# Moving the residual passes, the last two groups' order and the yr buffers in a fused attention and mixture-of-experts kernel

## What is computed

```python
h = _layernorm(x) * (1 + ca) + sa
q = h @ Wq;  Q = K = elu(q) + 1;  V = q / L
Z = 1 / (Q . Ksum + eps)
msg = (Q KV Z) * L @ Wm                       # linear attention, 8 heads of 16
a = h + _layernorm(msg, g1, b1)
a = a + _layernorm(relu(msg @ W1) @ W2, g2, b2)
x = x + ga * a
h = _layernorm(x) * (1 + cb) + sb
x = x + gb * experts(h)                       # 8 experts, top-512 tokens each, gelu FFN
```

## Times and profile before

| | us |
|---|---|
| median of 3 runs (310.49 to 312.85) | 312.84 |
| the profiled execution's own time | 311.66 |
| its span in the trace | 309.9 |

### The profile page before, as it was taken

How to read it: one execution, slowest core, us unless ns; L and a number is a source line. 1 busy time by engine, 2 the same in 40 slices (tenths; PEclk the granted TensorE clock), 3 DMA queues, 4 the chain that set the end, 5 groups by cost and what they waited for, 6 DMA issues and landing times.

```text
span 309.9 us, 4483 instructions
## 1 busy us (share of the span) xinstructions
PE 177.5 (57%) x1035; PEld 145.2 (47%) x1035; DVE 200.9 (65%) x701; ACT 98.5 (32%) x338; POOL 161.0 (52%) x229
## 2 busy tenths in 40 slices
PE   0878896596798895351112033527754574588730
PEld 0546684575586585351001022426644464577520
DVE  3789839949999988658897997013533253346660
ACT  1189843144265463115564002002221121222200
POOL 8645278917555334406991006770076665735552
PEclk9999997778699799555555555755995765758995
DMA  6940000000100000002662003432243333324210
GB/s 156 257 132 2 1 0 0 2 0 1 36 0 1 2 1 0 2 0 68 188 186 69 0 0 120 121 118 69 79 118 96 101 107 97 119 78 121 93 36 17
DMA packets 21721, 20.08 MB, mean 65 GB/s; under 512 B 2624, under 2 KB 19008, under 8 KB 21696
## 3 DMA queue, kind: packets, MB, share of 16 engines
q1 hardware_dynamic: 18144, 13.24, 14.7%
q0 software_dynamic: 2560, 6.30, 6.7%
q10 hardware_dynamic: 992, 0.27, 0.9%
HBM read 13.51 MB, written 6.29 MB: 64 GB/s over the span
## 4 chain that ended last, share of the span: by engine, by line
DVE 33%; PE 29%; another core or an unknown queue 13%; POOL 8%; issue 7%; ACT 6%; DMA 1%; DVEq 1%; POOLq 1%; ACTq 0%
PE pH L773 9%; DVE x_sb L965 6%; DVE hT L1044 5%; PE pQ L782 4%; POOL yr L244 3%; PE pH L675 3%; DVE bn L817 2%; ACT u L534 2%; PE pQ L668 2%; PE pQ L685 2%; POOL rs L244 2%; DVE xn L825 2%; PE pQ L567 2%; ACT x_sb L530 1%
## 5 line engine op out<-in xcount | busy, mean ns | idle before, releaser
L773 PE MATMUL pH<-x_sb,hid 128*128 (+1 forms) x156 | 35.9, 366 | 36.1 <-ACT x_sb L530 26.3
L373 POOL DMA_INDIRECT out_dram<-u,gidx x32 | 32.1, 1005 | 41.8 <-DVE u L1178 31.5
L369 POOL DMA_INDIRECT xn<-table_dram,gidx x32 | 33.6, 1051 | 33.2 <-DVE gidx L1138 23.8
L1166 DVE SCALAR_TENSOR_TENSOR h<-pQ,wslot,h 128x128 f32 (+1 forms) x39 | 13.7, 351 | 57.4 <-PE pQ L782 21.5
L773 PEld LDWEIGHTS pH<-x_sb,hid 128*128 128x128 f32 x156 | 27.1, 246 | 43.4 <-issue 43.4
L534 ACT ACTIVATE u<-pH 128x256 f32<-128x256 f32 x39 | 15.0, 384 | 80.7 <-remote 36.4
L782 PE MATMUL pQ<-ew,u 128*128 (+1 forms) x156 | 31.4, 337 | 3.9 <-issue 2.6
L782 PEld LDWEIGHTS pQ<-ew,u 128*128 128x128 f32 x156 | 27.6, 249 | 5.0 <-issue 4.7
L965 DVE SCALAR_TENSOR_TENSOR x_sb<-u,yr,x_sb 128x128 f32<-128x128 f32 x64 | 24.6, 445 | 4.4 <-POOL yr L244 4.1
L479 ACT ACTIVATE sqj<-pQ 128x128 bf16<-128x128 f32 x64 | 16.9, 278 | 28.4 <-POOL yr L244 12.3
L243 POOL TENSOR_SCALAR ve<-mv 128x4 f32<-128x4 f32 x16 | 3.3, 205 | 36.5 <-DVE mv L820 36.3
(11 more groups left out here) (275 smaller groups left out, 441.2 us busy)
## 6 DMA issues: line engine op xcount, KB each, us to landing
hid<-in_L_ffn_W_dram SPq DMA_DIRECT2D x39, 128.0 KB
x_sb<-in_L_attn_x_dram SPq DMA_DIRECT2D x8, 256.0 KB, 6.5
table_dram<-x_sb SPq DMA_DIRECT2D x8, 256.0 KB, 2.8
table_dram<-h SPq DMA_DIRECT2D x8, 256.0 KB, 2.3
ew<-in_L_ffn_W_dram SPq DMA_DIRECT2D x2, 512.0 KB, 7.6
xn<-table_dram,gidx POOLq DMA_INDIRECT x32
out_dram<-u,gidx POOLq DMA_INDIRECT x32
wmod_sb<-in_L_wmod_dram SPq DMA_DIRECT2D x1, 384.0 KB, 4.9
```

The costliest lines, as they stand in the source:

```text
L369: gp.indirect_dma_start(row[:, t % R, :], None, table[:, :], bass.IndirectOffsetOnAxis(gidx[:, t:t + 1], 0), bounds_check=B * L - 1, oob_i ...
L373: gp.indirect_dma_start(out.rearrange("b l d -> (b l) d"), bass.IndirectOffsetOnAxis(gidx[:, t:t + 1], 0), o_sb[:, t % RO, :], None, bound ...
L773: mm = te.matmul(pH[i % 2][:, f * P:(f + 1) * P], wcur[:, i % RW, f * P:(f + 1) * P], xt[:, bass.ds(i - e, 1), :], start=True, stop=True)
```

## The change

The residual passes are placed anew. POOL now does groups 0, 1, 2, 3, 4 and 7: acc(0) and acc(1) stand behind qprime(1), and then acc(2), acc(3), acc(4), acc(7) at the ends of steps 2 to 5. DVE does group 5 ahead of the last v_feat of the first stage and group 6 behind v_z(0). In the last steps DVE does x1(7) before xn3(6), POOL does yrs(7) before rs3(6), and PE does lg(6) before tx3(7). ssq, yv and yr have four buffers in place of two, with the waits to match.

```diff
-POOLACC = 5
+POOL_RES = (0, 1, 2, 3, 4, G - 1)
+RY = 4
...
             def acc(g):
                 b = g // GB
-                if g:
-                    gp.wait_ge(S["acc_done"], g)
+                k = POOL_RES.index(g)
+                if k:
+                    gp.wait_ge(S["acc_done"], k)
...
-            gp.wait_ge(S["rows_done"], 1)
-            gp.wait_ge(S["xn1"], G)
-            acc(0)
...
-                if g >= 2:
-                    gp.wait_ge(S["x1_done"], g - 1)
+                if g >= RY:
+                    gp.wait_ge(S["x1_done"], g - RY + 1)
...
             for s in range(G + 6):
                 if s < G:
                     qprime(s)
+                if s == G + 2:
+                    yrs(G - 1)
                 if 0 <= s - 4 < G:
                     rs3(s - 4)
-                if 0 <= s - 3 < G:
+                if 0 <= s - 3 < G - 1:
                     yrs(s - 3)
-                if s + 1 < POOLACC:
-                    acc(s + 1)
+                if s == 1:
+                    gp.wait_ge(S["rows_done"], 1)
+                    gp.wait_ge(S["xn1"], G)
+                    acc(0)
+                if 0 <= s - 1 < len(POOL_RES) - 1:
+                    acc(POOL_RES[s])
...
             def a_square(g, k, ready, done):
                 act.wait_ge(S[ready], g + 1)
-                if g >= 2:
-                    act.wait_ge(S["yr_done"], g - 1)
+                if g >= RY:
+                    act.wait_ge(S["yr_done"], g - RY + 1)
...
+                if s == G + 5:
+                    p_lg(G - 2)
                 if 0 <= s - 6 < G:
                     p_tx3(s - 6)
...
-                if 0 <= s - 7 < G:
+                if 0 <= s - 7 < G and s != G + 5:
                     p_lg(s - 7)
...
                 if s == G - 1:
                     v_kvt(0)
+                    v_acc(5)
...
-                if 1 <= s <= G - POOLACC:
-                    v_acc(POOLACC + s - 1)
+                if s == 0:
+                    v_acc(6)
+                if s == G + 3:
+                    v_x1(G - 1)
                 if 0 <= s - 5 < G:
                     v_xn3(s - 5)
-                if 0 <= s - 4 < G:
+                if 0 <= s - 4 < G - 1:
                     v_x1(s - 4)
```

More of the change, by code:

```diff
@@ L97, in build @@
         z = sb("z", [P, 2, GT * H]); qp = sb("qp", [P, 2, W]); qT = sb("qT", [P, 2, W])
-        hid = sb("hid", [P, 2, 2, W]); ssq = sb("ssq", [P, 2, 2 * GT]); yv = sb("yv", [P, 2, 2 * GT]); yr = sb("yr", [P, 2, 2 * GT])
+        hid = sb("hid", [P, 2, 2, W]); ssq = sb("ssq", [P, RY, 2 * GT]); yv = sb("yv", [P, RY, 2 * GT]); yr = sb("yr", [P, RY, 2 * GT])
         u1 = sb("u1", [P, 3, GT, D]); u2 = sb("u2", [P, 2, GT, D]); t2 = sb("t2", [P, GT, D]); t1 = sb("t1", [P, GT, D])
@@ L335, in yrs @@
                 gp.wait_ge(S["sq2"], g + 1)
-                if g >= 2:
-                    gp.wait_ge(S["x1_done"], g - 1)
-                rsqrt(yr[:, g % 2, :], ssq[:, g % 2, :], yv[:, g % 2, :], 1.0 / D, LN_EPS, 2 * GT).then_inc(S["yr_done"], 1)
+                if g >= RY:
+                    gp.wait_ge(S["x1_done"], g - RY + 1)
+                rsqrt(yr[:, g % RY, :], ssq[:, g % RY, :], yv[:, g % RY, :], 1.0 / D, LN_EPS, 2 * GT).then_inc(S["yr_done"], 1)
             def rs3(g):
@@ L475, in a_square @@
                 act.wait_ge(S[ready], g + 1)
-                if g >= 2:
-                    act.wait_ge(S["yr_done"], g - 1)
+                if g >= RY:
+                    act.wait_ge(S["yr_done"], g - RY + 1)
                 for t in range(GT):
                     last = act.activation(sqj[:, g % 2, k * GT + t, :], pQ[k][:, t * D:(t + 1) * D], ACT.Square,
-                                          accum_out=ssq[:, g % 2, k * GT + t:k * GT + t + 1])
+                                          accum_out=ssq[:, g % RY, k * GT + t:k * GT + t + 1])
                 last.then_inc(S[done], 1)
@@ L908, in v_kvt, with v_acc @@
                 dve.tensor_tensor(kvt[:, b, :], kv_bank(b), same16[:, :], ALU.mult).then_inc(S["kvt_done"], 1)
+            def v_acc(g):
+                b = g // GB
+                dve.wait_ge(S["rows_done"], 1)
+                link(dve.tensor_tensor(t2[:, :, :], xn[:, g], row4(rA[:, b, :]), ALU.mult))
+                link(dve.tensor_tensor(t2[:, :, :], t2[:, :, :], row4(rD[:, b, :]), ALU.add))
+                dve.tensor_tensor(bgroup(x_sb, g), bgroup(x_sb, g), t2[:, :, :], ALU.add).then_inc(S["acc_late"], 1)
+                dve.wait_ge(S["acc_late"], g - 4)
             for s in range(G + 1):
@@ L939, in v_relu @@
                 dve.tensor_scalar(hid[:, g % 2, 1, :], pH1[:, :], 0.0, None, ALU.max).then_inc(S["relu1"], 1)
[L941 to L946, removed]
             def v_u1(g):
@@ L959, in v_x1 @@
                 dve.wait_ge(S["yr_done"], g + 1)
-                if g < POOLACC:
-                    dve.wait_ge(S["acc_done"], g + 1)
+                if g in POOL_RES:
+                    dve.wait_ge(S["acc_done"], POOL_RES.index(g) + 1)
                 for u, n in ((u1[:, g % 3], 0), (u2[:, g % 2], GT)):
@@ L964, in v_x1 @@
                         x1 = x_sb[:, g * GT + t, :]
-                        last = dve.scalar_tensor_tensor(x1, u[:, t, :], yr[:, g % 2, n + t:n + t + 1], x1, ALU.mult, ALU.add)
+                        last = dve.scalar_tensor_tensor(x1, u[:, t, :], yr[:, g % RY, n + t:n + t + 1], x1, ALU.mult, ALU.add)
                     if n == 0:
```

## The result

| | before | changed |
|---|---|---|
| median of 20 runs, us | 312.71 (310.44 to 314.11) | 314.75 (312.90 to 316.78) |
| the profiled execution's own time, us | 311.66 | 314.16 |
| its span, us | 309.9 | 312.4 |
| DVE's mx starts (end of the middle stage), us | 137.22 | 139.12 |
| the experts' first gather on POOL starts, us | 187.39 | 189.09 |

The ratio of the changed kernel to the one before is 1.0076, with a 95% interval of 1.0049 to 1.0103: it is 2.0 us slower, which is less than 1%. The middle stage ends 1.9 us later. The search behind it takes 50.0 instead of 50.2 us, and the rest of the 2.5 us between the two spans lies in the experts' stage, 123.3 instead of 122.5 us. All ratios here leave out executions that took over 1.5% longer than the fastest of their kernel; in experiment E11 these are three of six.

The account below looks back on a forecast made before the run. The middle stage's chain of waits through DVE, POOL and PE was taken as the bound: start -2.8, passes beside x1 +6.4, tail -0.8 make +2.8 us, so 314.5 to 315.6, stated as 315.0 us; range 312.3 to 317.8 us.

Parts of the forecast that it names:

- the ring: Middle stage, DVE and POOL: x1(g), its stats, rs3(g) and yrs(g+1) wait in turn; what x1 takes, the ring takes.
- The passes behind yr(1) and yr(2) cost 6.4 us: Middle: x1(1) and x1(2) meet a pass on POOL and take 6.28 instead of 3.10 us each; bounds 6.2 to 6.5.
- The start gives 2.8 us: Up to x1(0): y2(0) ends at 64.3 us, as POOL takes back most of DVE's gain; bounds 1.1 to 5.1 us.
- the clock's return: Start, on PE: full clock returns 4 to 6 us after 56.6, so y2(0) ends at 64.0 to 65.1 us.
- acc(0) no longer beside DVE's pass costs nothing, the pass fits: First stage, DVE: group 5's pass takes 2.1 us within a 2.75 us wait for exp, without POOL's acc(0) beside it.
- The tail gives 0.8 us: Stage's end: x1(7) ends 2.7 us earlier, but PE's logit work at half clock keeps only 0.8; bounds 0 to 4.0.
- x1(7)'s start: Tail, on DVE: x1(7) starts at 123.8 instead of 126.56 us, within 0.1 us of u2(7)'s end.
- The four buffers do nothing: Buffers of ACT's squares and POOL's yrs: waits two groups back vanish, costed at nothing and gaining nothing.
- the slow clock: Rival on PE: the chain to y2(0) keeps its 7.60 us, the tail gives nothing; +5.3 us, 317.5 us; chance 0.20.
- the clock that stays up: Rival on PE: 2.4 GHz from tq(2) on; +0.5 us, 312.7 us, or 309.5 with a full-clock tail; chance 0.20.
- a ring that is bound elsewhere: Rival in the middle: POOL's yrs(2) waited for squares rather than rs3(1); time 312 us; chance 0.03.
- the ports held by DVE: Rival in the middle: x1's operations make POOL's passes wait, the middle costs nothing; about 309 us; chance 0.05.

Follow-up runs that it names:

- E11: The kernel before with only x1(7) ahead of xn3(6) and yrs(7) ahead of rs3(6); ratio to the kernel before 0.988.
- E1: The changed kernel without the residual passes of groups 4 and 7, so its output lacks them; ratio to the kernel before 0.985.
- E2: The changed kernel with POOL starting the passes of groups 4 and 7 only when x1(1), x1(2) are done; ratio to the kernel before 1.008.
- E7: The changed kernel with qp(4) to qp(7) waiting until x1(0) to x1(3) are done; ratio to the kernel before 1.001.
- E6: The changed kernel with POOL's pass of group 1 behind qp(2) and that of group 2 behind qp(3); ratio to the kernel before 0.996.
- E10: The changed kernel with acc(0) ahead of POOL's loop again, as in the kernel before; ratio to the kernel before 0.990.
- E4: The changed kernel with PE's tail order as before, tx3(7) ahead of lg(6); ratio to the kernel before 1.006.
- E5: The changed kernel with all three tail orders (DVE, POOL, PE) as before; ratio to the kernel before 1.014.
- E3: The changed kernel with two buffers for ssq, yv and yr instead of four; ratio to the kernel before 1.010.

## Why the prediction was right

The time, 314.75 us, lies 0.25 us from the 315.0 forecast, and the case is the forecast one. That it came so near is luck. The sum gave +2.8 us at the stage's end, where 1.9 us were measured: the start gave 1.1 us and a turn of the ring 0.4 us more than forecast, and the tail 0.7 us less. Outside the stage, where the forecast had nothing, another 0.6 us was added. What is more than luck is the largest term, the two passes beside x1, which came to within 0.1 us. Point by point:

- *The passes behind yr(1) and yr(2) cost 6.4 us.* Measured +6.34 over the three turns, x1(1) and x1(2) at 6.27 us each. E1 confirms what the stalls are, E2 that the ring has no room for a pass in another form either. The one reservation is E1's end, which moved by 4.7 us: part of the gain goes to ACT's squares when PE runs at half clock, so the term holds for adding the stalls, and not in full for taking them away.
- *The start gives 2.8 us.* Measured 3.9. The rows up to y1(1) came as worked out (qp(2) at 55.19 for 55.4, tq(2) at 56.30 for 56.6, y1(1) at 58.07 for 58.4). The term that was mis-sized is the clock's return: the granted clock was 0.50 from 56 to 59 us and 0.84 in the next, 3 us behind PE's restart and not 4 to 6, so y2(0) ended at 63.23 for 64.3. This, too, is partly luck: in E1 and E7, with the same work up to there, the clock came back between 5 and 7 us behind the restart. The mechanism, that POOL takes back what DVE gains, is shown by E6 and E10.
- *acc(0) no longer beside DVE's pass costs nothing, the pass fits.* The pass fits (38.46 to 40.59, ahead of featT at 41.37). But the text weighed the stalls on DVE that moving acc(0) avoids (a pass of 4.9 us, 4.1 in E10) and not what it costs on POOL by itself; E10 shows that this one move costs 4.2 us of the start and saves DVE 2.0 us, of which the 0.8 us of idle time ahead of featT would have hidden a part. The sum was right since it went by POOL's order as a whole.
- *The tail gives 0.8 us.* Measured 0.07. The orders act as worked out: lg(6) ahead of tx3(7) loses 1.2 us (E4), x1(7) ahead gains 1.3 us (E4 against E5, and E11). The mis-sized step is x1(7)'s start, 4.82 us behind x1(6)'s instead of 4.3, and 0.6 us behind u2(7)'s end where the prediction said 0.1: y2(7) took 3.04 us, as the clock fell during it, where it took 2.02 us before, and the squares ended late. In E2 and E7, with the same orders and y2(7) at 2.02 us, the tail takes 16.94 us, which is the 0.8 us.
- *The four buffers do nothing.* E3 shows it.
- *A turn the prediction didn't have.* x1(4) to x1(5) took 7.05 instead of 7.49 us, a gain of 0.44: POOL waited there for squares before, and no longer.

None of the rivals came: not the slow clock, not the clock that stays up, not a ring that is bound elsewhere (the turns from x1(1) and x1(2) grew by what x1 did, 3.18 and 3.18 us), and not the ports held by DVE. The last is excluded by x1(0) to x1(2): POOL's pass started 0.07 us ahead of x1 each time (66.46, 77.47, 88.48), and four of eight x1 operations waited.

What stays open is why PE's clock fell during y2(7) in some kernels and not in others. The idle time ahead of it was 1.87 us in the kernel before, where it stayed up, and 1.73 us in the changed one, where it fell between 120 and 121 us (y2(7) had started at 119.98). With the same 1.73 us it stayed up through y2(7) in E2, E5 and E7, fell during it in E1, E3, E4 and E11, and just ahead of it in E6 and E10.

## What to carry to other kernels

When work is moved on one engine to spare another a stall, ask what now stands behind it on its own engine. Here one edit moved work out of an idle time of POOL, where it was free, into the chain, and two more put it where each turn of a ring between two engines had no room. In such a ring, put side work behind the instruction that it collides with and beside those that it doesn't (qp beside bn was free, beside x1 it cost 0.8 us each). Two edits can cancel: x1(7) drawn ahead gave 1.3 us, and lg(6) ahead of tx3(7), once x1(7) stood there, lost 1.2 of them.

## What the runs showed of the hardware

- VectorE's operations with two tensor inputs in SBUF and GpSimd's take turns instruction by instruction. Beside a run of POOL operations with gaps of 0.08 us, one waiting DVE operation gets through per POOL operation, for both sizes seen: x1's of 0.29 us and a pass's of 0.69 us. POOL's own operation grows from 1.27 to 1.60 us where DVE's are of 128x512, and stays at 1.27 us beside x1's of 128x128.
- Operations of POOL on 128x8, such as the power that makes yr (1.64 us), leave DVE's xn instructions alone (four in 1.02 to 1.11 us beside it, 1.12 us with POOL idle). DVE's operations that read PSUM (0.63 us for hid and 0.68 us for u beside a pass in the changed kernel) and its bn (0.87 us for four beside a pass in E2) aren't touched by passes on POOL. An operation on SBUF alone with one tensor input can be: kdiag takes 0.27 us in the kernel before and 1.37 us beside a pass in the changed one.
- Where PE restarted at half clock in the changed kernel, the clock came back after 3 us; in the kernel before, ahead of y2(0), after 6. In E7, which does the same work up to there as the changed kernel, it took 6 us as well.
